# Moving the last head's band and the near bias of the row maxima to TensorE, with one PSUM bank for the values and four for the maxima

## What is computed

```python
x = x + 0.5 * _L1_ffn_ref(_layernorm(x, axis=-1), ...)
x = x + _L1_attn_ref(_layernorm(x, axis=-1), ...)
x = x + 0.5 * _L1_ffn_ref(_layernorm(x, axis=-1), ...)

def _L1_attn_ref(x, Wq, Wk, Wv, Wo, rel, ln_gamma, ln_beta):
    xn = _layernorm(x, ln_gamma, ln_beta)
    q = proj(Wq) / math.sqrt(DH)          # 16 heads of 16
    k, v = proj(Wk), proj(Wv)
    scores = jnp.einsum('bhid,bhjd->bhij', q, k)
    dist = jnp.clip(i[:, None] - i[None, :], 0, MAX_REL)   # MAX_REL = 128
    scores = scores + rel[:, dist][None]
    scores = jnp.where(causal[None, None], scores, -jnp.inf)
    attn = jax.nn.softmax(scores, axis=-1)
    y = jnp.einsum('bhij,bhjd->bhid', attn, v)
    return x0 + y @ Wo.T
```

## Time and profile before

| | us |
|---|---|
| median of 3 runs | 2555.85 (2555.43 to 2562.52) |
| span of the profiled execution | 2554.8 |
| first to last score of the heads stage | 1688.9 to 2411.9 |

### The profile page before, as it was taken

One profiled execution on the slowest core, in us unless ns is written; L12 is line 12 of the kernel. 1 busy time (PEld: TensorE's weight loads), 2 busy tenths in 40 slices (PEclk: granted clock), 3 DMA queues, 4 the chain that ended last, 5 costly groups with the idle time before them and its releaser, 6 DMA issues.

```text
span 2554.8 us, 38679 instructions
## 1 busy us (share of the span) xinstructions
PE 2128.9 (83%) x12842; PEld 1592.0 (62%) x12842; DVE 1539.1 (60%) x4444; ACT 970.2 (38%) x1961; POOL 314.8 (12%) x298
## 2 busy tenths in 40 slices
PE   4589999957999956899999456578998998999846
PEld 2478888856788935788888335434445545555435
DVE  7744343446455577434343598576876776778287
ACT  4122232322333342232323334235556556555532
POOL 4320000031000044100000432311002002000000
PEclk8699999978999978999999657579999999999956
DMA  8110111020000031110110310422422422422001
GB/s 260 43 64 24 31 30 31 26 64 26 1 1 1 1 116 58 51 31 27 29 30 26 91 44 25 73 46 58 51 28 51 74 29 54 72 29 27 2 25 50
DMA packets 84036, 114.84 MB, mean 45 GB/s; under 512 B 12212, under 2 KB 73816, under 8 KB 80728
## 3 DMA queue, kind: packets, MB, share of 16 engines
q1 hardware_dynamic: 77416, 94.80, 17.0%
q0 software_dynamic: 6432, 17.57, 2.2%
HBM read 69.16 MB, written 43.17 MB: 44 GB/s over the span
## 4 chain that ended last, share of the span: by engine, by line
PE 61%; DVE 26%; ACT 5%; issue 4%; DMA 2%; POOL 2%; DVEq 0%; ACTq 0%; SPq 0%; POOLq 0%
PE psum L775 10%; PE psum L777 10%; PE psum L776 10%; PE psum L126 5%; PE psum L2298 4%; PE psum L128 4%; PE psum L127 4%; DVE mt L2186 3%; PE psum L2277 3%; PE psum L862 3%; DVE m L2174 2%; PE psum L2257 2%; DVE stats L160 2%; DVE m L2183 2%; DVE xn L185 2%
## 5 line engine op out<-in xcount | busy, mean ns | idle before, releaser
L2137 ACT ACTIVATE pt<-psum 128x512 f32<-128x512 f32 (+3 forms) x768 | 333.9, 492 | 274.9 <-DVE psum L2212 180.1
L740 DVE SCALAR_TENSOR_TENSOR h<-psum,xg,sg 128x128 f32<-128x128 f32 x592 | 166.7, 344 | 415.6 <-PE psum L862 415.6
L556 ACT ACTIVATE sg<-psum 128x512 f32<-128x512 f32 x180 | 107.7, 598 | 575.1 <-PE psum L777 575.1
L775 PE MATMUL psum<-w_hi,xt_hi 128*128 (+1 forms) x720 | 285.6, 397 | 33.7 <-DVE xt_lo L705 33.7
L776 PE MATMUL psum<-w_lo,xt_hi 128*128 (+1 forms) x720 | 283.8, 394 | 0.0
L777 PE MATMUL psum<-w_hi,xt_lo 128*128 (+1 forms) x720 | 283.7, 394 | 0.0
L2257 PE MATMUL psum<-ks,qs 96*128 96x512 bf16 (+3 forms) x768 | 235.5, 347 | 36.0 <-DVE m L2174 10.2
L2277 PE MATMUL psum<-qs,ks 99*128 99x512 bf16 (+3 forms) x768 | 239.0, 334 | 24.4 <-ACT pt L2137 18.8
L775 PE MATMUL psum<-w_hi,ht_hi 128*128 (+1 forms) x720 | 218.1, 303 | 0.2
L2186 DVE CUSTOM_DVE_ANT_0 mt<-psum,band_q 128x256 bf16<-128x256 f32 (+1 forms) x512 | 204.2, 399 | 18.3 <-PE psum L2257 8.1
L2281 PE MATMUL psum<-band,ident_r 128*128 128x256 f32 (+1 forms) x864 | 214.8, 337 | 0.0
(11 more groups left out here) (284 smaller groups left out, 4420.1 us busy)
## 6 DMA issues: line engine op xcount, KB each, us to landing
xg<-w_dram SPq DMA_DIRECT2D x54, 256.0 KB, 3.2
qk_scr<-parts SPq DMA_DIRECT2D x32, 384.0 KB, 2.5
qs<-qk_scr SPq DMA_DIRECT2D x96, 128.0 KB, 7.2
ks<-qk_scr SPq DMA_DIRECT2D x96, 128.0 KB, 7.8
xg<-rows_in SPq DMA_DIRECT2D x74, 132.0 KB, 2.1
rows_out<-yb SPq DMA_DIRECT2D x74, 128.0 KB, 1.7
x<-x_dram SPq DMA_DIRECT2D x4, 1024.0 KB, 8.6
out_dram<-x SPq DMA_DIRECT2D x4, 1024.0 KB, 4.5
```

The source lines that it names most:

```text
L740: ins = dve.scalar_tensor_tensor(out=h[i % 2][:, e, :], in0=u[:, e, :], scalar=xg[j % XSLOT][:, at:at + 1], in1=sg[i % 2][:, e, :], op0=AL ...
L775: pe.matmul(out, a[0], b[0], start=first, stop=False)
L2137: act.activation(pt[n % NPT][:, 0:q1 - q0], st_bank(n)[:, 0:q1 - q0], ACT.Exp).then_inc(*exped.up())
```

## The change

The fourth head gets its band from TensorE as the others do: `band` holds all four heads, `band_dve`, the add L2212, its semaphore and the special order of heads are gone. The maxima are packed: nine full banks of 512 columns for each head (`PACKS`) in place of twelve part-filled uses; in each bank the blocks' near columns get their bias from a bf16 identity matmul with `band_q`, accumulated in the bank, and VectorE does one plain reduction per bank with 1, 2 or 4 results. `m3` is one buffer with four places for each block, set once, and is reduced by three instructions. The values of both halves go to one bank in turn, so cells are ordered by half, and the first value matmul of a half waits until ScalarE has copied the other; the first cell has 256 columns and the second is done in two parts (`WIDENS`). The ring gets four banks (4 to 7), scores have 1 to 3, the values 0. The end of a unit's half (`y_turn`) comes as soon as its last value is in the list, within the unit. In the linear stages two `ulp` buffers are shared by the four sets.

```diff
-        TILES, QUADS, XTS = 2, 4, 2
+        TILES, QUADS, ULPS, XTS = 2, 4, 2, 2
...
-                            if c - QUADS + first > 0:
-                                act.wait_ge(*less_ok(c - QUADS + first))
-                            act.activation(of(c).ulp, of(c).e, ACT.Relu, scale=2.0 ** -23).then_inc(*ulp_ok.up())
+                            if c - ULPS + first > 0:
+                                act.wait_ge(*less_ok(c - ULPS + first))
+                            act.activation(ulp_of(c), of(c).e, ACT.Relu, scale=2.0 ** -23).then_inc(*ulp_ok.up())
...
-                self.band = sb(stack, "band", [P, 2, NHG, HP, 2 * P], F32R)
-                self.band_dve = sb(stack, "band_dve", [P, NHG, 2 * P])
+                self.ident_q = sb(stack, "ident_q", [P, P], BF16)
+                self.band = sb(stack, "band", [P, 2, NHG, HG, 2 * P], F32R)
...
-        CELLS = [(0, 0), (0, 1), (1, 0), (4, 1), (1, 1), (2, 0), (5, 1), (2, 1), (3, 0), (6, 1), (3, 1), (7, 1)]
-        NCELL = len(CELLS)
+        CELLS = [(2, 0), (0, 0), (1, 0), (3, 0), (0, 1), (1, 1), (6, 1), (2, 1), (3, 1), (7, 1), (4, 1), (5, 1)]
+        NCELL, WIDENS = len(CELLS), (0, 0)
...
+        MS = 4
+        ROW_AT = {0: 0, 6: 1, 2: 2, 4: 3, 1: 4, 3: 5, 5: 6, 7: 7}
+        PACKS = [([(7, 0, 512)], 512, 28, 1), ([(0, 0, 128), (6, 0, 384)], 128, 3, 1),
+                 ([(7, 512, 1024)], 512, 29, 1), ([(6, 384, 896)], 512, 7, 1),
+                 ([(5, 0, 512)], 512, 24, 1), ([(1, 0, 256), (5, 512, 768)], 256, 19, 6),
+                 ([(4, 128, 640)], 512, 13, 1), ([(2, 0, 384), (4, 0, 128)], 128, 9, 1),
+                 ([(3, 0, 512)], 512, 20, 1)]
...
-            per_u = HG * BT + 7
+            per_u = HG * NPACK + 7
...
+                later = conclude(u, placed)
...
+                    if ending is None:
+                        tail = later
+                        ending = next(tail, None)
                     order.extend(ending or [])
-                    if step % 3 == 0 and ending is None:
+                    if step % 3 == 0 and not ending:
...
-            mx_ring = Ring([u for u in order if u[0] in MX], [psum[:, 5 + i, :] for i in range(3)])
-            y_banks = [psum[:, c, :] for c in range(CB)]
+            mx_ring = Ring([u for u in order if u[0] in MX], [psum[:, 4 + i, :] for i in range(4)])
+            y_bank = psum[:, 0, :]
...
                             if j == LAST[c]:
-                                if u:
-                                    act.wait_ge(*y_turned(CB * (u - 1) + c + 1))
+                                if CB * u + c:
+                                    act.wait_ge(*y_turned(CB * u + c))
                                 act.wait_ge(*value(u * NCELL + cell + 1))
-                                act.activation(ys[:, c * BANK:(c + 1) * BANK], y_banks[c],
-                                               ACT.Copy).then_inc(*ys_ok.up())
+                                act.activation(ys[:, :], y_bank, ACT.Copy).then_inc(*ys_ok.up())
...
+                        if kind == "max":
+                            u, h, s = i
+                            pieces, wide, at, step = PACKS[s]
+                            n = BANK // wide
+                            if h == 0 and s == 0:
+                                dve.wait_ge(*(row_max(u) if u else max_zero(1)))
+                            dve.wait_ge(*max_score(nth[i] + 1))
+                            dve.tensor_reduce(m3[:, h, at:at + (n - 1) * step + 1:step],
+                                              mx_ring.bank((kind, i)).rearrange("p (n k) -> p n k", k=wide),
+                                              AXIS.X, ALU.max).then_inc(*part_max.up())
...
-                        elif kind == "score":
-                            n, j, c, h, q0, q1, b1 = cell_of(i)
-                            if near_of[i[1]] and h >= HP:
-                                at = st_bank(n)[:, 0:b1 - q0]
-                                dve.wait_ge(*score(n + 1))
-                                dve.tensor_tensor(at, at, band_dve[:, i[0] % NHG, q0 - j * P:b1 - j * P],
-                                                  ALU.add).then_inc(*biased.up())
...
+                            o = 0
+                            for t, c0, c1 in PACKS[s][0]:
+                                w = (t + 1) * P
+                                near = c1 == w
+                                ins = pe.matmul(bank[:, o:o + c1 - c0], qs[r][0:KS_ROWS, h, t * P:(t + 1) * P],
+                                                ks[r][0:KS_ROWS, h, c0:c1], start=True, stop=not near)
+                                if near:
+                                    bw = min(w, 2 * P)
+                                    ins = pe.matmul(bank[:, o + w - bw - c0:o + w - c0], tables.ident_q[:, :],
+                                                    band_q[:, u % NHG * HG + h, 2 * P - bw:2 * P],
+                                                    start=False, stop=True)
+                                o += c1 - c0
+                            ins.then_inc(*max_score.up())
...
-                            by_pe = near_of[cell] and h < HP
+                            near = near_of[cell]
...
-                            if u and j == FIRST[c]:
-                                pe.wait_ge(*ys_ok(CB * (u - 1) + c + 1))
+                            if CB * u + c and j == FIRST[c]:
+                                pe.wait_ge(*ys_ok(CB * u + c))
                             pe.wait_ge(*exped(first + HG))
...
+                            edges = [q0, 2 * P, BANK] if (j, c) == WIDENS else [q0, (c + 1) * BANK]
+                            for lo, hi in zip(edges, edges[1:]):
+                                for h in range(HG):
+                                    slot = pt[(first + h) % NPT]
+                                    ins = pe.matmul(y_bank[h * MQ:h * MQ + DH + 1, lo - c * BANK:hi - c * BANK],
+                                                    v1[b % 2][:, j, g * HG + h, :], slot[:, lo - q0:hi - q0],
+                                                    start=(j == FIRST[c]), stop=(j == LAST[c]))
```

More of the change, by code:

```diff
@@ L31 @@
 NHG = HEADS // HG
-HP = HG - 1
 MQ = 32
@@ L1957, in conclude @@
                 b, g = divmod(u, NHG)
-                while not all(("value", (u, max(i for i, x in enumerate(CELLS) if x[1] == c))) in placed
-                              for c in range(CB)):
+                for c in range(CB):
+                    while ("value", (u, CELLS.index((LAST[c], c)))) not in placed:
+                        yield []
                     yield []
-                yield []
-                for t4 in range(CB):
-                    yield [("y_turn", CB * u + t4)]
+                    yield [("y_turn", CB * u + c)]
                 if g < NHG - 1:
@@ L2012, in heads_order @@
                     order.append(("load", u + NR))
-                order.extend(sum(tail, []))
-                tail = conclude(u, placed)
+                tail = later
             for tokens in due:
```

154 lines of the change are left out of this document (51 added, 103 removed).

## The result

| | before | after |
|---|---|---|
| median of runs, us | 2558.03 (2555.43 to 2562.52) | 2585.59 (2582.25 to 2587.20) |
| ratio to before | | 1.0102, 95% interval 1.0084 to 1.0120 |
| span of the profiled execution | 2554.8 | 2585.5 |
| first max matmul to first score (prologue) | 38.3 | 34.0 |
| first to last score (stretch) | 722.8 | 749.6 |

The change makes the kernel 1.0% slower: 27.6 us by the medians of four runs each, 30.7 by the profiled spans. The parts from the fourth row down are read from the starts of TensorE's instructions in one execution each; the stretch is cut at the first score of each unit as in the earlier trace rows, whose first window begins 1.6 us ahead of the first max matmul.

The account below looks back on a forecast made before the run. TensorE was taken as the bound. Stretch +17 us (740 for 723), prologue -3.5 and tail 0 made +13.5: 2568.3 us for the profiled 2554.8, or 2569 as a median; range 2530 to 2606.

Parts of the forecast that it names:

- prologue: Unit 0's maxima before the first score: 3.5 us less (0 to 5), by 36 packs at 0.60 us on VectorE.
- stretch: First to last score: 705 us of TensorE work plus 35 idle, 740 us for 723, +17.
- rival 2: Heads: TensorE's idle time stays at 80 us, with long waits for `ys` and `pt`; +58.5, 2614 us; chance 0.20.
- upper bound of that term: VectorE's maxima: if pieces cost like separate reductions, 4 us a unit more, still under 31 of some 40.
- in plain units hardly any: Units without a projection: hardly any TensorE idle time stays, with a third of 102 us, 35, left in the stretch.
- three small reductions in place of one: nothing: End of a unit's maxima: the extra reductions move within engines that have slack, costing nothing.
- Hidden: Single value bank: the wait for ScalarE's copy (607 ns) lies under TensorE's other work; if not, at most 19 us.
- what VectorE ended goes: Stretch: idle time of TensorE ended by VectorE goes with its lighter load, as do exp waits from L2212.
- the ring of four: Maxima and projections: a held bank would hold up the fourth use after it, not the third; no gain counted.
- One memset less: nothing: Heads: dropping a memset moves within engines that have slack, gaining nothing.
- Rival 1: Heads: TensorE's idle time goes nearly wholly, down to 10 us; -11.5, 2544 us; chance 0.20.
- Rival 3: Heads: TensorE has headroom, added matmuls hide and VectorE sets the pace, 4.3 us a unit less; 2483 us; chance 0.07.

Follow-up runs that it names:

- experiment 4: Kernel before with one value bank, cells by half, four maxima banks, earlier half turn, shared `ulp`: 2549.48 us; with three maxima banks 2565.93.
- (6): experiment 4's kernel with the memset of the row maxima's buffers only at each buffer's first use: 2531.60 us; with the maxima's turn later too, 2527.17.
- (7): experiment 4's kernel with the fourth head's band on TensorE: 2556.86 us (single run); with the memset only at first use as well, 2543.08.
- Experiment 1: Changed kernel with the near-bias matmuls of the maxima left out: 2538.75 us (single run).
- experiment 2: Changed kernel with the maxima's turn put between the next unit's first packs: 2574.06 us; with units 0 and 1 left as they were, 2567.53.
- experiment 3: Changed kernel with a ring of three banks for the maxima in place of four: 2584.02 us, ratio 1.0092.
- experiment 8: Changed kernel with GpSimd's low part of the band kept one head wide in four table pairs: 2585.22 us (single run).

## Why the prediction was right and wrong

The direction was right and the size was half of what came: +13.5 forecast, 27.6 measured, 30.7 between the profiled spans. The measured 2585.6 us lies just above the 2554 to 2584 that the forecast gave itself, at the lowest edge of rival 2's share. The runs give a ladder for the stretch, each step one part of the change on top of those before it:

| kernel | stretch | step | plain unit | time |
|---|---|---|---|---|
| before | 722.8 | | 37.1 | 2558.0 |
| + bank part (experiment 4) | 712.5 | -10.3 | 36.0 | 2549.5 |
| + no memset for each unit (6) | 697.8 | -14.7 | 36.0 | 2531.6 |
| + fourth head's band on TensorE (7) | 703.5 | +5.7 | 37.1 | 2543.1 |
| + packed maxima, no near bias (1) | 702.5 | -1.0 | 38.0 | 2538.8 (single run) |
| + near bias on TensorE: the changed kernel | 749.6 | +47.1 | 41.4 | 2585.6 |

The last but one step takes in all that goes with the packs, the turn's new place in the order among it; its -1.0 is no more than two profiles of the same heads differ by. By the terms of the forecast's sum, in the profiled executions:

| term | forecast | measured |
|---|---|---|
| ahead of the heads | 0 | +2.8 |
| prologue | -3.5 | -4.3 |
| stretch | +17 | +26.8 |
| tail (0.3) and last linear stage (5.0) | 0 | +5.3 |
| sum (rounded) | +13.5 | +30.7 |

**The bound** was named rightly. Experiment 1 shows that work added to TensorE is paid in full, while the packing, which is what relieves VectorE, gave 1.0 us of the stretch and made the plain unit 0.9 longer.

**The work** was sized rightly too. Near bias: 0.11 or 0.12 from start to start, 3.4 us a unit for 3.3, 47.1 in the stretch for 50. With no stall at the turn a plain unit takes 39.8 for 39.6. *VectorE*: 27.1 us busy where about 27 stood among the signs; the bank pieces with several results cost 690 ns, no more than one result, so the upper bound of that term was not needed.

**The step that failed is "in plain units hardly any" idle time.** It was argued from VectorE's lighter load, and a lighter load says nothing about a latency. The turn needs the last pack, its reduction and the rows; the change made that chain longer (0.69 and 0.41 against an add-and-max of 0.41, its 0.08 read and a row reduction of 0.25) and, by the new order, put two scores in front of the turn where a value group and two scores had been. I had written "three small reductions in place of one: nothing". TensorE stands about 1.0 us there in each plain unit, and 1.8 us of 41.4 are idle in all. Seven plain units came to 291.6 us for 277.2 forecast (7 x 39.6), 14.4 more. That is more than the stretch's whole surplus of 9.8 over the forecast's 17; the pairs and the ends came out 4.6 better. The total idle of the stretch, 749.6 - 705 = 45 us, is within the 20 to 50 of the forecast but not where it was put: the turn and the copies took 18 us between them. In the ladder the stall shows as the 0.9 us that the packs add to a plain unit (37.1 to 38.0) though they take work off VectorE and none is added to TensorE; the wait for the turn is 0.9 us in that 38.0.

**The idle time came near its forecast by errors that offset each other.** Some 57 us of it went (102 to 45), where the forecast had 67 go, with VectorE's lighter load and the exps' waits for its adds. By the ladder 27 of the 57 belong to the bank part (10.3, and the 2 us of work that it adds) and to the memset (14.7), which the forecast gave nothing, and 26 to the fourth head's band (32 us of work for 5.7 of stretch). The packs, which relieve VectorE most, gave 1, and the near bias 3. The band's part came as forecast, by the waits that it ends; that the rest came out near is luck.

**The single value bank.** "Hidden" holds for the value matmuls: L2273 waited for no copy, and TensorE's waits for exps fell from 18.8 to 5.9 us in the stretch, so rival 2's signs did not appear. The transposes behind the copy were not thought of. They come some 0.3 us too early in thirteen places and 4.2 once, 8.2 in all; in part this follows from the turn, since without the stall (experiment 2) it is 6.4, with the 4.4 at the end of unit 0 in it.

**The fourth head's band** was costed at 32 us of work, and "what VectorE ended goes" was left to the sum of idle time. In two settings it cost 6 us of stretch, and 7.4 and 11.5 by the times (16 by the ratios of the second), so between half and four fifths of it were paid back by the waits it ends. My first and second expectation of it were both too high by the medians.

**Banks.** The forecast named the ring of four and then gave it nothing; on the old maxima it is worth 16 us. On the packed maxima it is worth nothing (experiment 3). "One memset less: nothing" was wrong as well: on the bank part it is worth 14.7 us of stretch and 18 of time (21 by the ratios). In the pair of the earlier trace rows VectorE waited for that memset only 1.6 us, for 6.9 with the bank part alone, so it could not be seen at that size in the kernel before. Its waits in such a pair (total, times, longest) were, before:

```profile
DVE m L2174 <- POOL m L2112: 1.6, 1, 1.6
```

And with the bank part alone, with TensorE's wait for the maxima that follows from it:

```profile
DVE m L2176 <- POOL m L2116: 6.9, 2, 4.9
PE psum L2259 <- DVE m L2176: 4.7, 4, 2.2
```

What a memset for each unit would cost on the packed maxima, and what one less would gain on the kernel before, was not tried.

**The last linear stage.** Its 5 us are not shown to be the change's. The change does touch this stage: it has two `ulp` buffers in place of four. But VectorE's instructions keep their places in it to within 0.3 us until 110 us in, and ScalarE's waits ahead of `ulp` are all for `power`, so no wait for a shared buffer shows. After that the granted clock differs. Two windows of the end, of the kernel before and then of the changed one:

```profile
2530.00:2540.00 10.00, 8.37 (x41) 6.64 (x41) 7.67 (x10) 1.91 (x3) 0.00 (x0) 0.75 0.32 107
2540.00:2554.00 14.00, 8.35 (x42) 6.65 (x42) 4.01 (x7) 1.16 (x3) 0.00 (x0) 0.69 0.21 70
```

```profile
2555.70:2565.70 10.00, 7.96 (x34) 6.27 (x32) 7.67 (x10) 1.77 (x3) 0.00 (x0) 0.67 0.31 105
2565.70:2579.70 14.00, 13.29 (x49) 10.90 (x49) 3.38 (x6) 1.28 (x3) 0.00 (x0) 0.50 0.00 0
```

Both pairs of windows lie equally far (100.5 us) behind the start of the stage. The clock is 0.75 and 0.69 of full speed before, 0.67 and then 0.50, the lower level of 1.2 GHz, after. Over the thirteen kernels of this study that have this stage with two buffers it took 125.1 to 130.4 us, 128.1 on average. The profiled execution of before (125.3), the only one with four, lies at the low end of that range and that of after near its top. No run has the change with four buffers, so a small cost of the shared ones is not excluded. Part of the 2.8 us ahead of the heads can be chance as well, by the starts in experiment 8. Without both the change costs 23 us in the profile; the medians say 27.6, and where the rest lies the profiles do not show.

**The prologue** came out at -4.3 for -3.5. The clock granted in it was 0.70 for 0.50 before, the denser TensorE that the prediction kept for its range; but without the near bias, with less work for TensorE, the prologue took 33.8 at 0.50. VectorE was busy 28.8 us in the one and 28.6 in the other, so its length goes with VectorE and not with the clock.

**The signs.** ScalarE's exps no longer wait for VectorE, VectorE is at 27, the bias matmuls take 0.11 to 0.12 from start to start, the pairs changed by -1.3, -3.2 and -1.7 us: as forecast, the second pair by a little more. Plain units of 39 to 40.5 us without a gap of 1 us: missed, and that miss makes the surplus of the stretch.

**The rivals.** Rival 1 (idle down to 10 us) fell at the turn. Rival 2 (idle stays at 80) was too pessimistic with 80 for 45, and neither of its two waits came; the result lies at its edge for another reason. Rival 3 fell by experiment 1.

## What to carry to other kernels

On a nearly full engine, count for each step that waits for a result how much of its own work lies between the producer and itself, and compare that with the latency of the chain; a lower busy share of the other engine does not shorten it, and moving the waiting step by a few places can give back most of what an edit costs (18 of 27.6 us here). Small initialising instructions on an engine whose in-order queue also carries late work should be done once, outside the loop: a memset of 0.18 us for each unit cost 18 us. Work put on the bound engine was paid in full where it ended no wait (the near bias, 47 of 50 us); where it ended one, half or more came back (the band, 32 us of work).

## What the hardware showed

A VectorE reduction of a full PSUM bank takes 0.69 us whether it writes one, two or four results per partition. Groups by form of the changed kernel's stretch (busy us, mean ns, idle before):

```profile
L2154 DVE TENSOR_REDUCE m<-psum 128x1 f32<-128x512 f32 x360 | 242.0, 688 | 111.3 <-PE psum L2224 54.5 <-PE psum L2228 51.5
L2154 DVE TENSOR_REDUCE m<-psum 128x4 f32<-128x512 f32 x120 | 82.8, 690 | 44.9 <-PE psum L2224 42.9 <-DVE mean_var L162 0.2
L2154 DVE TENSOR_REDUCE m<-psum 128x2 f32<-128x512 f32 x60 | 41.4, 690 | 29.0 <-PE psum L2228 28.2
```

A GpSimd subtraction of 128 x 512 in place of 128 x 256 (1.27 for 0.73 us) lengthened a VectorE multiply of only 32 columns from 0.47 to 1.01 us. Towards the end of the last linear stage TensorE was granted 0.69 in the profiled execution of before and 0.50 in that of after, though the two had done the same work (208 matmuls) in the stage's first 100 us, at 0.57 and 0.59; what decides between them no run shows.
